# A mixture-of-experts stage whose tiles are transposed by DMA instead of by TensorE

## The reference

```
x = x + cross_attention(layernorm(x), ctx)            # 16 heads
x = x + quantised_ffn(layernorm(x))                   # 704 hidden, 8-bit fake quantisation
x = x + mlstm_attention(layernorm(x), ctx, ctx)       # 4 heads
x = x + moe(layernorm(x))
# moe: 8 experts, each token goes to its best 2, weights w_i normalised to sum 1
h   = silu(x @ w1[i]) * (x @ w3[i])                   # 256 -> 1024
out = sum_i w_i * (h @ w2[i])                         # 1024 -> 256
```

## Time and profile before

| | us |
|---|---|
| median of 3 runs (lowest, highest) | 857.44 (856.37, 859.57) |
| the profiled execution, its own time | 855.12 |
| its span | 853.4 |
| expert stage, first gate/up matmul to the end of the last tile's gate and up | 449.88 to 829.25 |
| tile interval, no new expert near | 9.2 to 9.6 |

### The profile page before, as it was taken

The page is one execution under the profiler, slowest core; times in us unless marked ns, Lnnn a source line. Parts: engine busy times, 40 slices in busy tenths (PEclk is TensorE's granted clock), DMA queues, the critical chain, the costliest instruction groups (busy, mean ns, idle before and its releaser), DMA issues.

```text
span 853.4 us, 18930 instructions
## 1 busy us (share of the span) xinstructions
PE 684.8 (80%) x4518; PEld 465.6 (55%) x4519; DVE 525.0 (62%) x1359; ACT 411.0 (48%) x815; POOL 278.0 (33%) x390
## 2 busy tenths in 40 slices
PE   2999999885856776477318989898989998989992
PEld 2788887763324335466304656565656565656661
DVE  5577789986767434888784454646464555564441
ACT  1466665555877254454125544554354545543430
POOL 3111111110436103534212273536354354453321
PEclk9799999987879897555558999999999999999996
DMA  8100000003000005111370614343431525431213
GB/s 264 32 13 12 12 18 6 7 1 99 1 0 0 3 17 199 34 29 25 113 239 14 175 31 129 73 126 73 119 82 30 169 44 159 127 70 25 37 20 111
DMA packets 45643, 58.41 MB, mean 68 GB/s; under 512 B 13296, under 2 KB 39216, under 8 KB 45072
## 3 DMA queue, kind: packets, MB, share of 16 engines
q1 hardware_dynamic: 38128, 47.79, 17.4%
q0 software_dynamic: 7488, 10.31, 7.4%
HBM read 145.90 MB, written 11.80 MB: 185 GB/s over the span
## 4 chain that ended last, share of the span: by engine, by line
PE 49%; DVE 19%; issue 13%; POOL 7%; ACT 3%; DMA 3%; DVEq 2%; POOLq 1%; ACTq 1%; SPq 0%
PE psum L1009 17%; PE psum L1031 7%; PE psum L723 3%; POOL region L663 3%; PE psum L1022 3%; PE psum L707 3%; PE psum L730 3%; PE psum L914 2%; PE psum L743 1%; PE psum L762 1%; PE psum L712 1%; PE psum L845 1%; DMA region<-xrow_dram,next_token 1%; DVE region L1380 1%; PE psum L904 1%
## 5 line engine op out<-in xcount | busy, mean ns | idle before, releaser
L1009 PE MATMUL psum<-region 128*128 x936 | 216.8, 382 | 15.7 <-POOL pause_p L665 6.4
L1009 PEld LDWEIGHTS psum<-region 128*128 128x128 bf16 x936 | 91.9, 98 | 117.2 <-issue 28.6
L1031 PE MATMUL psum<-region 128*128 x936 | 112.3, 278 | 6.1 <-DVE region L1895 5.6
L1283 ACT ACTIVATE region<-psum 128x512 f32<-128x512 f32 x78 | 46.6, 598 | 118.4 <-PE psum L1009 118.4
L1031 PEld LDWEIGHTS psum<-region 128*128 128x128 bf16 x936 | 92.0, 100 | 21.0 <-issue 8.8
L1865 DVE TENSOR_TENSOR region<-psum,region 128x512 f32<-128x512 f32 x78 | 53.9, 691 | 71.8 <-ACT region L1283 69.3
L633 POOL TENSOR_TENSOR pause_p<-minus_half 128x1 f32<-128x1 f32 x37 | 7.1, 193 | 188.9 <-DVE next_token L1881 188.1
L645 POOL DMA_INDIRECT sum_dram<-region,tok_idx x39 | 62.0, 1589 | 6.6 <-issue 6.3
L530 POOL TENSOR_TENSOR region<-region,pair_mask 128x256 f32<-128x256 f32 x32 | 18.9, 613 | 138.1 <-ACT region L1076 138.1
L1304 ACT ACTIVATE pause_a<-one_col 128x1 f32<-128x1 f32 x117 | 23.7, 202 | 80.9 <-issue 66.3
L1895 DVE TENSOR_TENSOR region<-psum,region 128x1024 bf16<-128x1024 f32 x39 | 47.7, 1222 | 16.9 <-ACT region L1291 16.9
(11 more groups left out here) (304 smaller groups left out, 1361.0 us busy)
## 6 DMA issues: line engine op xcount, KB each, us to landing
region<-in_L_ffn_w SPq DMA_DIRECT2D x117, 1024.0 KB
region<-in_ctx SPq DMA_DIRECT2D x32, 128.0 KB, 2.4
region<-neg_max_dram SPq DMA_DIRECT2D x4, 1024.0 KB, 4.8
xrow_dram<-region SPq DMA_DIRECT2D x1, 2080.0 KB, 8.0
x_sb<-in_x SPq DMA_DIRECT2D x4, 512.0 KB, 6.2
region<-in_ctx SPq DMA_DIRECT2D x2, 1024.0 KB, 6.9
sum_dram<-x_sb SPq DMA_DIRECT2D x1, 2048.0 KB, 7.5
region<-in_L_ffn_w_down SPq DMA_DIRECT2D x1, 704.0 KB, 8.8
```

The lines of the kernel that those rows point to most:

```text
L1009: last = mm(psum[:, 2 * f + n, :], (xT_lo if xl else xT_hi)[:, p, k, :], weights_at(place, wl, n, k * F1 + f * FH, FH), start=(i == 0), st ...
L1031: last = mm(psum[:, 7, 0:D], (hT_lo if hl else hT_hi)[:, f, :], weights_at(place, wl, 2, f * D, D), start=(i == 0), stop=(i == 3 * (F1 // ...
L1283: act_fn(sil_d[:, f, :], psum[:, 2 * f, :], ACT.Silu).then_inc(sil_d_ready, 1)
```

## The change

The transposes of x and h leave TensorE. The rows of x are stored as bf16 pairs: high part in the first 256 bf16 values, low part in the next 256, made by ACT (high) and POOL (low, new `row_low`) before `xrow_dram` is written. The output of SwiGLU is split the same way, a half of 512 columns at a time, in rows: ACT makes the high part (`h_high`), DVE the low part (`h_low`), both from `h_d` in SBUF. SP then issues one transposing DMA for x of a tile (128 x 512 bf16 to 4 blocks of 128 x 128) and two for h (each 128 x 1024 bf16 to 8 blocks). The results `xT_d` and `hT_d` have two buffers each.

SP's program is written out for all 39 tiles and its order changes: per tile t the two h transposes, then loads of part 0 for tile t+4, part 1 for tile t+3 and part 2 for tile t+2 (one part of a new expert per tile), then the x transpose of tile t+2.

```diff
+            def transpose_x(t):
+                sp.wait_ge(xg_loaded[t % 2], 16 * (t // 2) + 16)
+                if t >= 1:
+                    sp.wait_ge(xT_loaded, 16 * t)
+                if t >= 2:
+                    sp.wait_ge(gu_done, 2 * t - 2)
+                sp.dma_start_transpose(xT_d[:, t % 2, :, :], xg_pair[:, t % 2, :]).then_inc(xT_loaded, 16)
+            def transpose_h(t, f):
+                sp.wait_ge(h_low_ready, 2 * t + f + 1)
...
+                sp.dma_start_transpose(hT_d[:, t % 2, f, :, :], h_pair[:, t % 2, f, :]).then_inc(hT_loaded, 16)
...
-            load_step(0, 0)
-            with sp.Fori(0, (NT - 5) // 2) as i:
-                load_step(2 * i + 1, 1, inner=True)
-                load_step(2 * i + 2, 0, inner=True)
+            for t in range(NT):
+                transpose_h(t, 0)
+                transpose_h(t, 1)
+                if t + 4 < NT:
+                    load_part(0, t + 4, t % 2)
+                if t + 3 < NT:
+                    load_part(1, t + 3, 1 - t % 2)
+                if t + 2 < NT:
+                    load_part(2, t + 2, t % 2)
+                    transpose_x(t + 2)
@@ POOL, router @@
+            def row_low(b):
+                pool.wait_ge(dt_evac, b + 1)
+                nc.gpsimd.tensor_tensor(xrow_pair[:, b, D:2 * D], xn_r[:, b % 2, :], xrow_pair[:, b, 0:D],
+                                        ALU.subtract).then_inc(xrow_low_ready, 1)
@@ PE, tile_step @@
-                pe.wait_ge(xT_low, t + 1)
+                pe.wait_ge(xT_loaded, 16 * t + 16)
                 gate_up_half(t, p, 0, place, inner)
+                gate_up_half(t, p, 1, place, inner)
                 if inner or t >= 1:
-                    h_transposes(t - 1, 1 - p)
-                gate_up_half(t, p, 1, place, inner)
-                if inner or 0 < t < NT - 1:
-                    x_transposes(t + 1, 1 - p, loads_next, inner)
-                if inner or t >= 1:
-                    down_d(t - 1, place_of(t - 1), inner)
+                    down_d(t - 1, 1 - p, place_of(t - 1), inner)
@@ ACT @@
+            def h_high(t, p, f, inner=False):
+                act.wait_ge(h_d_ready, 2 * t + f + 1)
...
+                act_fn(h_pair[:, p, f, 0:FH], h_d[:, p, f * FH:(f + 1) * FH], ACT.Copy).then_inc(h_high_ready, 1)
@@ tile_step of ACT @@
                 silu_d(t, 0)
+                h_high(t, p, 0, inner)
                 if inner or t + 2 < NT:
                     weights_high(0, t + 2, p, pair + 2, inner)
...
                 silu_d(t, 1)
+                h_high(t, p, 1, inner)
...
@@ DVE @@
+            def h_low(t, p, f):
+                dve.wait_ge(h_high_ready, 2 * t + f + 1)
+                tt(h_pair[:, p, f, FH:2 * FH], h_d[:, p, f * FH:(f + 1) * FH], h_pair[:, p, f, 0:FH],
+                   ALU.subtract).then_inc(h_low_ready, 1)
```

More of the change, by code:

```diff
@@ L181, in build @@
         neg_max_dram = nc.dram_tensor("neg_max_dram", (B * H1, P), F32, kind="Internal").ap()
-        (top, oh1, oh2, rt, rt2, rbase, incl, incl2, v1, v2, m12, e2, w12, etiles, eend, eend2, eoff,
-         iota_e, iota_t, tcmp, te, tchg, tcum, tslot, slots_f, xg, xT_hi, xT_lo, sil_d, h_d,
-         hT_hi, hT_lo, y_d, w_col, stage) = lay(
+        (xT_d, hT_d, top, oh1, oh2, rt, rt2, rbase, incl, incl2, v1, v2, m12, e2, w12, etiles, eend, eend2, eoff,
+         iota_e, iota_t, tcmp, te, tchg, tcum, tslot, slots_f, xg, sil_d, h_d,
+         h_pair, y_d, w_col, stage) = lay(
             region1,
+            (BF16, 2, 2 * KT, P), (BF16, 2, 2, 2 * FH // P, P),
             (F32, B, E), (F32, B, E), (F32, B, E), (F32, B, E),
@@ L349, in build @@
         part_low = [sem(f"part_low{i}") for i in range(3)]
-        tx_done = sem("tx_done")
-        xT_high = sem("xT_high")
-        xT_low = sem("xT_low")
+        xT_loaded = sem("xT_loaded")
+        xrow_low_ready = sem("xrow_low_ready")
         gu_done = sem("gu_done")
@@ L454, in _ @@
             sp.wait_ge(xrow_routed, 1)
+            sp.wait_ge(xrow_low_ready, B)
             sp.wait_ge(route_consts, 12)
@@ L1008, in gate_up_half, with down_d @@
                     for i, (k, (xl, wl)) in enumerate((k, pair) for k in range(KT) for pair in PAIRS):
-                        last = mm(psum[:, 2 * f + n, :], (xT_lo if xl else xT_hi)[:, p, k, :],
+                        last = mm(psum[:, 2 * f + n, :], xT_d[:, p, xl * KT + k, :],
                                   weights_at(place, wl, n, k * F1 + f * FH, FH), start=(i == 0), stop=(i == 3 * KT - 1))
                 last.then_inc(gu_done, 1)
-            def x_transposes(t, p, loads, inner=False):
-                pe.wait_ge(xg_loaded[p], 16 * loads)
-                for k in range(KT):
-                    last = tr(bank(6, 4, P)[:, k, :], xg[:, p, k * P:(k + 1) * P], ident[:])
-                last.then_inc(tx_done, 1)
-            def h_transposes(t, p):
-                pe.wait_ge(h_d_ready, 2 * t + 2)
-                for f in range(F1 // P):
-                    last = tr(bank(4, F1 // P, P, count=2)[:, f, :], h_d[:, p, f * P:(f + 1) * P], ident[:])
-                last.then_inc(th_done, 1)
-            def down_d(t, place, inner=False):
-                pe.wait_ge(hT_low, t + 1)
+            def down_d(t, p, place, inner=False):
+                pe.wait_ge(hT_loaded, 32 * t + 32)
                 pe.wait_ge(part_low[2], t + 1)
@@ L1030, in down_d @@
                 for i, (f, (hl, wl)) in enumerate((f, pair) for f in range(F1 // P) for pair in PAIRS):
-                    last = mm(psum[:, 7, 0:D], (hT_lo if hl else hT_hi)[:, f, :], weights_at(place, wl, 2, f * D, D),
+                    half, c = divmod(f, FH // P)
+                    last = mm(psum[:, 7, 0:D], hT_d[:, p, half, hl * (FH // P) + c, :], weights_at(place, wl, 2, f * D, D),
                               start=(i == 0), stop=(i == 3 * (F1 // P) - 1))
@@ L1311, in tile_step @@
                 silu_d(t, 0)
-                if inner or t >= 1:
-                    h_high(t - 1)
+                h_high(t, p, 0, inner)
                 if inner or t + 2 < NT:
                     weights_high(0, t + 2, p, pair + 2, inner)
-                if not inner and t == 0:
-                    x_high(1, 1)
                 silu_d(t, 1)
-                if inner or 0 < t < NT - 1:
-                    x_high(t + 1, 1 - p)
+                h_high(t, p, 1, inner)
                 if inner or t + 2 < NT:
@@ L1876, in route_of @@
                 tt(w_col[:, p:p + 1], w_col[:, p:p + 1], xg[:, p, D + 3:D + 4], ALU.add)
-                dve.wait_ge(tx_done, t + 1)
+                dve.wait_ge(xT_loaded, 16 * t + 16)
                 last = nc.vector.tensor_copy(tok_idx[:, p:p + 1], xg[:, p, D:D + 1].bitcast(U32))
```

90 lines of the change are left out of this document (37 added, 53 removed).

## The result

The changed kernel takes 1028.32 us (median of 4 runs, 1025.51 to 1030.54), the kernel before 858.51 beside it. The ratio is 1.198, 95% interval 1.194 to 1.202. The forecast was 951 with 893 to 1010 around it: the sign is right, the size is not, and the time lies outside the range. The profiled execution has a span of 1028.8 where before had 853.4.

A forecast was written before the change was run, and what follows sets the result against it. TensorE, busy 354.5 of 381 us, bounded the expert stage; then the late x transpose would. Later start, 19 x 20.75, new experts 56, clock 13, last halves 5.35 and tail put the profiled execution at 949, the median at 951 us; range 893 to 1010.

The forecast's parts named there:

- S(0): Start of the first expert tile's gate/up products, behind the router: forecast to move from 449.88 to 453.2.
- 19 pairs, as if no expert were new: Expert stage: every two tiles take 20.75 us, 10.4 a tile instead of 9.2 to 9.6.
- clock, booked apart: TensorE behind the idle gaps at new experts: matmuls slower by 1.7 to 2.0 us, 7 times, 13 us in all.
- 7 new experts: At each change of expert, later marker and x transpose behind a 1 MB load: 8 us a time, 56 in all.
- tail: After the last tile's gate/up products: h reaches the down product 6.8 us behind their end, against 6.1 before; booked as 1.
- The x transpose as the edge: On SyncE, x of tile t+2 stands behind GpSimd's marker and three loads, landing too late: 10.4 us a tile.
- The first rival: Expert stage: the x transpose comes in time and TensorE stays the bound, 819 us; chance 0.06.
- the gap of 2.3 us: TensorE's idle time in each plain tile: slow clock there costed at nothing, 36 us put into the range.
- step 1 of the chain: From the end of gate/up products to GpSimd's marker: 7.4 us plus 1.1, sum 8.5, bounds 0.5 and 1.5.
- h transposes "at nothing": SyncE's h transposes: h ready 3.0 us after the gate/up products, needed 10.4 after, so in time at no cost.
- DMA engines as the bound, 998: Expert stage: transposes in 256-byte pieces at 62 ns a packet make 13.3 us a tile, about 998 us; chance 0.15.
- sixteen `row_low` mostly lie in its idle time: Router: GpSimd's subtractions of 0.61 us are mostly hidden; only the last delays the constants, top-2 search 1.8 late.

The follow-up runs named there:

- h_psum: The changed kernel with the SwiGLU product written to two PSUM banks instead of h_d in SBUF: 1026.11 us, ratio 1.201.
- x_first_old_loads: The changed kernel with weight loads in the order of before and the x transpose of t+2 issued ahead of them: 944.64 us, ratio 1.108.

## Why the prediction was wrong, point by point

The error is 81.8 us on the profiled execution (forecast 853.4 + 93.6 = 947.0, span 1028.8). From the same rows:

| term | forecast | measured | worked out from |
|---|---|---|---|
| S(0) later by | 3.3 | 11.1 | first gate/up 460.94 |
| 19 pairs, as if no expert were new | 19 x 20.75 = 394 | 19 x 23.7 = 450 | end of products to that of the tile after next, 23.5 to 24.1 where no new expert is near |
| clock, booked apart | 13 | 38, in the pairs and new experts | 20 tiles of 6.3 to 8.2 against 5.35 |
| 7 new experts | 56 | 88 | 543.5 from S(0) to E(38), less 450 and 5.3 |
| tail | 1 | 0.2 | 24.3 behind E(38), before 24.15 |

- **The x transpose as the edge: right.** The chain from E over L695 and three loads is in the trace step by step, for tile 5: L695 9.8 where I had 8.5, SyncE 3.6 (3.8), landing 2.5 (2.9). The first rival (TensorE bound, 819) fell.
- **What a pair needs: the step that failed is "in plain tiles the gap of 2.3 us ... I leave it at nothing".** The cold matmuls cost 2.0 a pair in the mean (7.3 against 5.35; 2.5 in the pair above), two thirds of the 2.95 by which a pair was too short. I had taken the idle time as 2.3 in front of each tile; by the same sum that is 20.75 less 16.2 = 4.55 a pair, and it came in one piece, 5.6 to 7.2 in front of every second tile. The row at 835.36 had shown slow matmuls behind 2.46 us of idle time; I should have followed the nearest row. The other third is step 1 of the chain, mis-sized: from E to L695 I had 1.1 more than before, with 1.5 as its upper bound, and it is 2.4 more (9.8 for 7.4). In the pair above 0.5 of it is the SiLU that starts late behind ScalarE's own markers, and 0.5 is GpSimd's marker, 1.26 long instead of 0.76; in `h_psum`, where VectorE's `h_low` reads PSUM, the marker is 0.76 again. SyncE and the landing were 0.1 and 0.3 shorter than I had them.
- **Round a new expert: the step that failed is that the changed order of loads had no term.** I counted a load's 1 MB ahead of the transpose (2.4) and SyncE's time, and never asked who waits for part 2 while SyncE waits for L695. By the runs this order costs 98 us where nothing hides it, 20 to 65 in the changed kernel, and the rows of tile 8 above show it: 22.9 from E to L695 where I had 16.1. In the trace of before ScalarE's waits name no load at all; that they had one tile of SyncE's step to spare, and that the change takes it away, was there to be worked out.
- **h transposes "at nothing": wrong.** They are hidden in the changed kernel as it is, since x is later still. With x mended they are what TensorE waits for (72.5 us), and the versions with only h by DMA are 50 slower than before, of which a part, not measured by itself, is the order that I gave GpSimd and VectorE. The forecast asked whether h is in time under a 10.4 us tile, not what it costs when the first wait is gone.
- **DMA engines as the bound, 998: nearer than I rated it, for another reason.** The traffic with SyncE's time for it costs 29 us, not 143. The packets are there: 141712 - 38128 = 103584 more, 885 for each transposing DMA, close to the pieces of 256 bytes that I had counted (853). But they are not 62 ns each: the queue's time on the engines grows from 17.4% of 853.4 us to 27.7% of 1028.8 on 16 engines, which is 21 ns for each of them. In the expert stage the two data queues fill 48% of the engines (36.6 and 11.4). The Trainium skill ("VectorE: DVE Perf Modes", The three transpose paths) has 1309 ns for a 128x128 bf16 block; four blocks landed 2.5 us behind issue here, eight in 3.0 to 3.1, so blocks do not run in turn and the measurement decides. Its other rule ("Advanced Engine Details and Errata", X-Bar Transpose), as fast as regular DMAs, agrees: 2.5 beside 2.4 for a plain 128 KB load.
- **Router: the step that failed is "sixteen `row_low` mostly lie in its idle time".** They lie in GpSimd's idle time and in VectorE's working time. The row of the changed kernel, beside GpSimd's subtraction at 414.47, 0.68 long:

```profile
414.54 0.89 DVE L1697 TENSOR_TENSOR region<-region 128x256 f32<-128x256 f32 x1 [0.45 <-POOL region L613]
```

0.89, where it takes 0.42 alone. Both of its inputs are in SBUF, and it ends only when GpSimd is done. Where VectorE reads one input from PSUM, as `h_low` in `h_psum`, the mean stays at 692. The Trainium skill ("SBUF — State Buffer", Who interferes with whom) says that a `tensor_tensor` with both inputs in SBUF contends with GpSimd's reads, and calls the port pair that the two share an exclusive lock. The traces agree: 4.85 for 0.69, 2.90 for 0.16, 0.89 for 0.42. That rule spoke against this change, which moves `h_low` from PSUM to SBUF and adds GpSimd work; I had weighed two rules on the transfer and not this one.

What holds the 170 us, as far as the runs tell: the order of SyncE's step (loads and x) 84; the places of GpSimd's low part, VectorE's row numbers and h in SBUF 43 (944.64 to 901.53); h by DMA with all traffic and the router about 51, of which the router is 12 and idle transposes are 29, each measured in the kernel before. These parts were not measured as a sum of independent terms, and two of them (18 and 20 alone, 84 together) plainly are none. The slow clock's 38 us are not a part of their own but lie within them: with the 84 undone (`x_first_old_loads`) only 3 tiles are slow, 2.6 us in sum.

## What to carry to other kernels

When a change adds a transfer to an in-order queue, write down for every entry of that queue both what it waits for and who waits for it; an entry that is skipped still holds the queue until its wait is over, and one late semaphore passes through each in-order engine behind it. Two chains that hide each other give back little when one is cut (18, 20) and much when both are (84), so a single undo that does little is no proof that the cause is elsewhere. When a sum yields idle time for TensorE, ask in how many pieces it comes, and look in the trace for matmuls behind a gap of that size. Work on two engines that read SBUF at once is not free parallel work: before work goes to an idle GpSimd, look at what VectorE does at that time and whether an operand of it is in PSUM.

## What the runs showed of the hardware

- A transposing DMA from SBUF to SBUF (128x512 bf16) is there 2.5 us behind its issue, 128x1024 in 3.0 to 3.1, and holds SyncE 1.2 us; behind one 1 MB load the first took 5.9 to 7.0, behind two 5 to 7.3.
- A VectorE operation with both inputs in SBUF that meets a GpSimd subtraction of 128x256 or 128x2048 does not end before it, however small: 0.89 for 0.42, 4.85 for 0.69, and a single column took 2.90 for 0.16. It is not so for each GpSimd operation: beside GpSimd's power of one column at 415.09 VectorE's L1699 of the changed kernel kept its 0.42.
- TensorE came back at a granted clock of 0.50 after 5.81 and after 13.30 us of idle time (24 matmuls in 7.82 and 7.98 instead of 5.35), and ran at 1.00 where other matmuls filled the gap (5.35).
